# Row gathers of a graph stage: five in flight in place of four

## The chip, the cores and the metric

One core of a Trainium2 chip runs the whole kernel in one launch. The time is device microseconds of one execution; three runs of the kernel before took 5215.01 to 5220.03 us, with a median of 5218.09.

## The reference

The input is 32 images of 64 channels and 48 x 48 pixels. Two layers follow one another, and each adds its result to its input.

```python
x = x + conv(ln_c(x), Wc, bc)             # per image: s = relu(xn^T xn)^2 over all pixel pairs; out = s applied to Wc x + bc
t = to_tokens(x)                           # 73728 tokens of 64 numbers
h = (ln_t(t) @ W_gat).reshape(M, HEADS, NUM_EXPERTS)
e = leaky_relu(a_src[src] + a_dst[dst])    # 262144 drawn edges and a loop at each node
alpha = exp(e - segment_max(e, dst)) / segment_sum(...)
agg = segment_sum(h[src] * alpha, dst) + b_gat
scores = layernorm(agg).mean over heads    # 4 experts, the best 2 taken, softmax weights
out = t + sum over experts of g * (gelu(x @ W1 + b1) @ W2 + b2)
```

The edges are sorted by destination on the chip, so that each maximum and each sum over a destination is a scan along a sorted row. For each edge the row of its source node (24 numbers: 16 of h, 4 of a_src, 4 of a_dst) has to be fetched by an index.

## The kernel before, in words

The program is written out by engine: each of PE, DVE, ACT, POOL and SP has its own list of instructions, and they meet on semaphores. Three parts follow one another.

- `weave` does the first 8 images and sorts the edges between their steps; `merge_nodes` merges the loops into the sorted edges. Drawn edges only name nodes of the first 8 images.
- `flow` does the other 24 images. Meanwhile POOL fetches the source rows of all edges. This is `gather_rows`: 2048 gathers (line 984), each of which takes 128 rows of 96 bytes from the table `htab_d` in HBM by 128 indices and puts them into the tile `rows`. 64 gathers make a chunk; 32 chunks alternate between two halves of `rows`. After the tenth gather of a chunk (`EARLY`) `store_rows` (line 963) writes the chunk before it to `raw_d` in HBM.
- At most `IN_FLIGHT` gathers may be on their way: gather t waits until gather t - IN_FLIGHT has landed (line 983). Gather t counts on semaphore `landed[t % IN_FLIGHT]`, so each place has its own. A store waits on all of them.

When 28 chunks are fetched, POOL waits for the end of the images (`img_done`, line 1730), which SP announces at line 1642, and then works through 32 segments. For each, `segment_rows` issues two large gathers: `got` (line 1724), the segment's edges from `raw_d`, and its neighbour `nb` (line 1726), rows of its nodes from `htab_d`. After each pair it does up to 13 (`PIECE`) of the 256 row gathers that are left; they last for 20 segments. `got` of segment k also waits until ACT has laid out the segment before the last (`a_got`).

For each segment ACT lays out `nb` and `got` (lines 2117 and 2118), and DVE runs the segment's scans, which end with the scan `S` (line 2519). Behind the last segment come a small correction (PE's transposes at lines 1924 and 1929, on semaphore `pe_tails`) and the last stage: for each image POOL fetches 18 times 128 rows (`R`, line 1769), DVE and ACT make gates of them, and PE runs the experts. The expert biases are transposed on PE at line 1919 as soon as the images are done, and DVE copies them at line 2453; they had a semaphore of their own, `pe_b`.

Of the kernel before, what the change touches and what calls it, by code (L numbers as in the profile page):

```python
# [25 lines left out]
FAR = 1.0e6  # L26
FIRST = 8
MIRROR = 40959
IN_FLIGHT = 4
EARLY = 10  # L30
OPENING = 48
KEPT = 49152
# [10 lines left out]
def kernel_program(nc, x, Wc, bc, Wg, att_s, att_d, b_gat, gamma, beta, W1, b1, W2, b2, edges, out):  # L43
# [32 lines left out]
    with ExitStack() as ctx:  # L76
# [7 lines left out]
        def sem(name):  # L84
            return ctx.enter_context(nc.semaphore(name))
# [32 lines left out]
        n.j_in = [sem("j_in0"), sem("j_in1")]  # L118
        n.landed = [sem(f"landed{f}") for f in range(IN_FLIGHT)]
        n.raw_out = [sem("raw_out0"), sem("raw_out1")]  # L120
# [25 lines left out]
        with ExitStack() as sorting:  # L146
            n.big = [sorting.enter_context(nc.sbuf_tensor(f"edges{i}", [P, 2, n.EC], F32)) for i in range(3)]
            weave(nc, n, Wc, bc, Wg, att_s, att_d, edges)
            with ExitStack() as merging:
# [9 lines left out]
                n.slots = mb("slots", [P, n.G * n.W], I32)  # L159
                merge_nodes(nc, n)  # L160
        flow(nc, n, Wc, bc, Wg, att_s, att_d, b_gat, gamma, beta, W1, b1, W2, b2)


# [794 lines left out]
def store_rows(pool, n, k):  # L958
    chunk = n.raw[n.CW:n.E + n.CW, :].rearrange("(k p j) c -> k p (j c)", p=P, j=n.GC)
    end = (k + 1) * n.GC  # L960
    for f in range(IN_FLIGHT):
        pool.wait_ge(n.landed[f], 16 * ((end - f + IN_FLIGHT - 1) // IN_FLIGHT))
    pool.dma_start(chunk[4 * n.G - 1 - k], n.rows[:, k % 2, :, :].rearrange("p j c -> p (j c)")).then_inc(n.raw_out[k % 2], 16)  # L963


def gather_rows(pool, n, t0, t1):
    GC, G, NK = n.GC, n.G, 4 * n.G
    for t in range(t0, t1):
# [11 lines left out]
        if j == 0 and k >= 2:  # L980
            pool.wait_ge(n.raw_out[k % 2], 16 * (k // 2))
        if t >= IN_FLIGHT:
            pool.wait_ge(n.landed[t % IN_FLIGHT], 16 * (t // IN_FLIGHT))
        pool.indirect_dma_start(out=n.rows[:, k % 2, j, :], out_offset=None, in_=n.htabx,  # L984
                                in_offset=bass.IndirectOffsetOnAxis(ap=n.idx[:, g % 2, 3 - c, j:j + 1], axis=0)).then_inc(n.landed[t % IN_FLIGHT], 16)
        if j == EARLY - 1 and k:
# [255 lines left out]
def flow(nc, n, Wc, bc, Wg, att_s, att_d, b_gat, gamma, beta, W1, b1, W2, b2):  # L1242
    B, C, NP, HE, NH, NX = n.B, n.C, n.NP, n.HE, n.NH, n.NX
# [33 lines left out]
    E, M, NT, HID = n.E, n.M, n.NT, n.HID  # L1277
# [19 lines left out]
    with ExitStack() as ctx, ExitStack() as early, ExitStack() as late:  # L1297
# [3 lines left out]
        def sem(name):  # L1301
            return ctx.enter_context(nc.semaphore(name))
# [7 lines left out]
        def ph(name, shape, dt=F32):  # L1310
            return late.enter_context(nc.sbuf_tensor(name, shape, dt))
# [69 lines left out]
        b1r = ph("b1r", [NX, HID])  # L1381
# [44 lines left out]
        up = [late.enter_context(nc.psum_tensor(f"up{i}", [P, 2, 512], F32)) for i in range(GROUP)]  # L1426
# [43 lines left out]
        pe_tails = sem("pe_tails")  # L1470
# [8 lines left out]
        r_free = sem("r_free")  # L1479
        r_in = [sem("r_in0"), sem("r_in1")]  # L1480
        v_set = sem("v_set")
        pe_b = sem("pe_b")
        v_gx = sem("v_gx")
        a_gx = sem("a_gx")
        v_gt = sem("v_gt")
# [287 lines left out]
        def _(pe):  # L1773
# [142 lines left out]
                tokens(B - 1, i)  # L1916
            pe.wait_ge(img_done, 1)
            pe.wait_ge(ew_in, 96)
            pe.transpose(up[0][0:HID, 0, 0:NX], b1r[:, :], n.ident[0:NX, 0:NX]).then_inc(pe_b, 1)
            pe.wait_ge(v_set, 1)  # L1920
            pe.wait_ge(v_tails, 1)
            for k in range(3):
# [41 lines left out]
        def _(act):  # L1964
# [165 lines left out]
                act.activation(state[:, k % 2, :, 0:NC5], S[:, :, :, :].rearrange("p h e j -> p j (h e)"), ACT.Copy)  # L2130
                act.activation(state[:, k % 2, :, NC5:RW], MF[:, :, :].rearrange("p h j -> p j h"), ACT.Copy).then_inc(a_rows, 1)
            for k in range(3):
                act.wait_ge(pe_tails, k + 1)
                act.activation(rt[:, k, :], turn_ps[:, k, :], ACT.Copy).then_inc(a_tails, 1)
            act.wait_ge(v_exp, NK + 1)
            act.activation(ea[:, :, :].rearrange("c a p -> c (a p)"), ex[:, :, :].rearrange("c a p -> c (a p)"), ACT.Exp).then_inc(a_exp, 1)
# [49 lines left out]
        def _(dve):  # L2186
# [262 lines left out]
            norm2(B - 1)  # L2449
            dve.wait_ge(img_done, 1)  # L2450
            dve.wait_ge(ew_in, 96)
            dve.wait_ge(pe_b, 1)
            dve.tensor_copy(b1t[:, :], up[0][0:HID, 0, 0:NX]).then_inc(v_set, 1)
            done = [1]

# [23 lines left out]
            for q in range(G):  # L2479
                par = q % 2  # L2480
                dve.wait_ge(g_in[par], 48 * (q // 2 + 1))
                for c in range(KCH):
                    k = q * KCH + c
# [52 lines left out]
            dve.wait_ge(a_exp, NK + 1)  # L2536
            step(dve.tensor_tensor(ea[:, 1, :], ea[:, 1, :], rt[:, 0, :], ALU.mult))
            dve.tensor_tensor_scan(So[:, 1:G * P + 1], ea[:, 0, :], ea[:, 1, :], 0.0, ALU.mult, ALU.add).then_inc(v_car, 1)
            dve.wait_ge(pe_tails, 4)
            step(dve.tensor_copy(carry[:, :, :, :], back_ps[:, :, :, :]))  # L2540
            dve.sem_inc(v_carry, 1)
            dve.wait_ge(fix_in, 16 * G)
# [154 lines left out]
```

## Time and profile before

| | |
|---|---|
| profiled execution | 5217.17 us |
| its span, first to last instruction | 5214.9 us |
| busy: PE, DVE, ACT, POOL | 67%, 76%, 65%, 56% |
| chain that ended last, by engine | POOL 39%, issue 14%, DMA 13%, DVE 10% |
| row gathers, line 984 | 2048, 2093.9 us busy, 1022 ns each |
| idle time of POOL before them | 663.8 us |

The span is what the profile sees; the 2.3 us around it belong to the launch. In the chain "issue" is time in which an engine waited for nothing that the profile shows, such as the fixed time between two of POOL's gathers, and a DMA's share is its time from issue to landing. The busy time of a gather on POOL ends when the gather is issued, not when its rows have landed. The idle time before an instruction is told with what ended it.

### The profile page before, as it was taken

The numbers are of one execution on the slowest core, as the hardware profiler recorded it, in microseconds if no ns is written. First come the engines' busy times: TensorE is split into PE (matmuls) and PEld (weight loads), VectorE is DVE, ScalarE is ACT, GpSimd is POOL, SyncE is SP. The second block draws the span as 40 slices with busy tenths as digits, with TensorE's granted clock in tenths as the row PEclk, the third lists the DMA queues.
The fourth block names the chain that finished last, engine by engine and source line by source line (L and its number), as shares of the span: only waits on it lengthen the run. The fifth ranks groups of instructions, "written<-read, shape, count | busy, mean of one in ns | idle before, by whom it ended". The sixth has DMA issues, their size and how long they took to land.

```text
span 5214.9 us, 70585 instructions
## 1 busy us (share of the span) xinstructions
PE 3470.7 (67%) x22687; PEld 1460.3 (28%) x22687; DVE 3969.3 (76%) x5512; ACT 3405.7 (65%) x4010; POOL 2917.5 (56%) x2937
## 2 busy tenths in 40 slices
PE   4888988600399999999999999940000017777777
PEld 1223333200144444444444444420000002222222
DVE  8998988997767767777767665635888948778777
ACT  4787978500587877787778777733555527666666
POOL 6000000048777777777777777777774147666661
PEclk9898999855699999999999999975555558899999
DMA  6100110002122222222222222233545526999997
GB/s 256 42 20 21 25 29 16 13 18 83 21 44 56 53 52 55 56 54 52 60 51 53 60 51 51 53 59 116 177 166 195 171 73 144 150 156 165 160 156 153
DMA packets 322231, 441.88 MB, mean 85 GB/s; under 512 B 185241, under 2 KB 251676, under 8 KB 321260
## 3 DMA queue, kind: packets, MB, share of 16 engines
q1 hardware_dynamic: 199504, 288.13, 21.1%
q0 software_dynamic: 105536, 148.61, 16.8%
q10 hardware_dynamic: 16896, 1.18, 0.2%
q8 instruction: 187, 3.06, 0.2%
q14 instruction: 108, 0.88, 0.1%
HBM read 252.35 MB, written 166.47 MB: 80 GB/s over the span
## 4 chain that ended last, share of the span: by engine, by line
POOL 39%; issue 14%; DMA 13%; DVE 10%; SPq 1%; PE 1%; ACT 0%; DVEq 0%; POOLq 0%; ACTq 0%
POOL rows L984 35%; DMA rows<-htab_d,idx 6%; DMA gs<-gates_d 5%; POOL R L1769 2%; DVE ms L2641 1%; DVE pairs L2648 1%; DVE S L2519 1%; SPq L1680 1%; DVE AD L2504 1%; DVE AE L2498 1%; POOL nb L1726 1%; DVE total L2650 0%; POOL got L1724 0%; PE ye L1941 0%; POOL raw_d L963 0%
## 5 line engine op out<-in xcount | busy, mean ns | idle before, releaser
L984 POOL DMA_INDIRECT rows<-htab_d,idx x2048 | 2093.9, 1022 | 663.8 <-issue 606.5
L2073 ACT ACTIVATE rel<-gram 128x1024 f32<-128x1024 f32 (+1 forms) x1080 | 1003.1, 933 | 350.5 <-PE gram L1885 344.1
L2418 DVE SCALAR_TENSOR_TENSOR s<-gram,rel 128x1024 f32<-128x1024 f32 (+1 forms) x720 | 793.3, 1117 | 559.9 <-ACT rel L2073 543.3
L1839 PE MATMUL acc<-s,gT 128*64 128x512 f32 (+1 forms) x4320 | 1031.4, 554 | 0.4 <-issue 0.4
L1885 PE MATMUL gram<-hl 128*64 128x512 f16 (+1 forms) x4320 | 798.2, 366 | 108.9 <-DVE s L2418 65.4
L1885 PE MATMUL gram<-hl,lh 128*64 128x512 f16 (+1 forms) x4320 | 788.1, 362 | 0.0
L1769 POOL DMA_INDIRECT R<-seg_d,nidx x576 | 591.0, 1026 | 194.2 <-issue 168.8
L1084 POOL IOTA slots<- 64x2048 int32 x1 | 1.8, 1832 | 974.1 <-POOLq L192 974.1
L1941 PE MATMUL ye<-hid,w 128*64 128x384 f32 x1536 | 353.7, 538 | 285.4 <-DVE ms L2641 166.5
L2165 ACT ACTIVATE hid<-up,b1t 128x768 f32<-128x768 f32 x384 | 335.7, 899 | 254.2 <-PE up L1953 226.2
L1924 PE MATMUL tailsT<-ident,tails 128*20 128x128 f32 x24 | 5.2, 412 | 731.2 <-DVE tails L2527 731.2
L910 ACT ACTIVATE w_s2r<-w_gram 128x1024 f32<-128x1024 f32 (+1 forms) x360 | 348.1, 967 | 93.9 <-PE w_gram L779 93.4
L316 DVE TENSOR_TENSOR edges<-edges 128x2048 f32<-128x2048 f32 (+1 forms) x186 | 370.7, 1993 | 46.6 <-ACT edges L939 40.9
L1885 PEld LDWEIGHTS gram<-hl 128*64 128x64 f16 x4320 | 251.5, 110 | 515.0 <-DVE s L2418 219.0
L1953 PE MATMUL up<-tne,w 64*128 64x384 f32 x1536 | 373.2, 565 | 7.8 <-DMA x2e<-x_d 7.1
L317 DVE TENSOR_TENSOR edges<-edges 128x2048 f32<-128x2048 f32 (+1 forms) x186 | 369.8, 1988 | 0.0
L753 PE MATMUL w_acc<-w_s2r,w_gT 128*64 128x512 f32 (+1 forms) x1440 | 364.3, 585 | 0.6 <-ACT w_s2r L892 0.6
L892 ACT ACTIVATE w_s2r<-w_s2r 128x1024 f32<-128x1024 f32 (+1 forms) x360 | 360.8, 1003 | 0.0
L2077 ACT ACTIVATE s<-rel 128x1024 f32<-128x1024 f32 (+1 forms) x360 | 349.7, 971 | 11.5
L1839 PEld LDWEIGHTS acc<-s,gT 128*64 128x64 f32 x4320 | 304.2, 139 | 156.7 <-issue 5.9
L2641 DVE SCALAR_TENSOR_TENSOR ms<-ye,b2c,gs 128x384 f32<-128x384 f32 x384 | 233.4, 614 | 135.8 <-DMA gs<-gates_d 97.5
L1885 PEld LDWEIGHTS gram<-hl,lh 128*64 128x64 f16 x4320 | 252.4, 111 | 271.8 <-issue 171.6
(372 smaller groups left out, 5404.8 us busy)
## 6 DMA issues: line engine op xcount, KB each, us to landing
gs<-gates_d SPq DMA_DIRECT2D x64, 1152.0 KB
rows<-htab_d,idx POOLq DMA_INDIRECT x2048
seg_d<-state SPq DMA_DIRECT2D x32, 996.0 KB, 4.2
raw_d<-w_zeros POOLq DMA_DIRECT2D x48, 512.0 KB, 23.2
raw_d<-rows POOLq DMA_DIRECT2D x32, 768.0 KB
tne<-tn_d SPq DMA_DIRECT2D x64, 288.0 KB
x2e<-x_d SPq DMA_DIRECT2D x64, 288.0 KB
out<-res SPq DMA_DIRECT2D x64, 288.0 KB, 8.4
```

The lines of the kernel that those rows point to most:

```text
L316: dve.tensor_tensor(lo, a, b, ALU.min)
L317: step(dve.tensor_tensor(hi, a, b, ALU.max))
L753: last = pe.matmul(acc[(b + c) % 2][j * C:(j + 1) * C, 0:w], gT[:, b % 2, 2 * k + j, :], s2(s)[:, j * w:(j + 1) * w], start=k == 0, stop=k ...
L892: act.activation(s2(s)[:, 0:2 * w], rel(s)[:, 0:2 * w], ACT.Square).then_inc(a_s2, 1)
L984: pool.indirect_dma_start(out=n.rows[:, k % 2, j, :], out_offset=None, in_=n.htabx, in_offset=bass.IndirectOffsetOnAxis(ap=n.idx[:, g % 2, ...
L1769: pool.indirect_dma_start(out=R[:, par, j, :], out_offset=None, in_=n.seg, in_offset=bass.IndirectOffsetOnAxis(ap=nidx[:, par, j:j + 1], a ...
L1839: last = pe.matmul(acc[(par + c) % 2][j * C:(j + 1) * C, 0:w], gT[:, par, 2 * k + j, :], s2[:, u % SLOTS, j * w:(j + 1) * w], start=k == 0 ...
L1885: last = pe.matmul(bank[h * C:(h + 1) * C, j, 0:w], word[:, par, first_pixel:first_pixel + C], hl[:, par, o:o + w], start=own_words, stop= ...
L1941: last = pe.matmul(y[i % 2][h * C:(h + 1) * C, 0:EW], w2[:, k, :], hid[:, i % GROUP, h, :], start=True, stop=True)
L1953: last = pe.matmul(up[i % GROUP][:, h, 0:EW], w1[rows_, k, :], tne[rows_, par, cp * EW:(cp + 1) * EW], start=True, stop=True)
L2073: act.activation(rel[:, t % RELS, 0:2 * w].rearrange("p (j x) -> p j x", j=2), gram[(par + t) % 2][:, :, 0:w], ACT.Relu, scale=1.0 / SPLIT ...
L2418: dve.scalar_tensor_tensor(halves(s2[:, t % SLOTS, 0:2 * w]), gram[(par + t) % 2][:, :, 0:w], 1.0 / SPLIT ** 2, halves(rel[:, t % RELS, 0: ...
```

## The change

The number of gathers in flight goes from 4 to 5. Each place keeps its own semaphore, so there is one more `landed`; the semaphore `pe_b` is taken away, and the transposed biases are counted as the first increment of `pe_tails`. Whoever counted on `pe_tails` waits for one more.

```diff
-IN_FLIGHT = 4
+IN_FLIGHT = 5
...
-        pe_b = sem("pe_b")
...
-            pe.transpose(up[0][0:HID, 0, 0:NX], b1r[:, :], n.ident[0:NX, 0:NX]).then_inc(pe_b, 1)
+            pe.transpose(up[0][0:HID, 0, 0:NX], b1r[:, :], n.ident[0:NX, 0:NX]).then_inc(pe_tails, 1)
...
-                act.wait_ge(pe_tails, k + 1)
+                act.wait_ge(pe_tails, k + 2)
...
-            dve.wait_ge(pe_b, 1)
+            dve.wait_ge(pe_tails, 1)
...
-            dve.wait_ge(pe_tails, 4)
+            dve.wait_ge(pe_tails, 5)
```

The instructions keep their order on every engine; only what they wait for differs. Around the first raw store POOL's list before reads as follows (line, operation, out<-in, partitions x elements):

```order
195 L984 DMA rows<-htab_d,idx 128x24 [waits landed0]
196 L984 DMA rows<-htab_d,idx 128x24 [waits landed1]
197 L963 DMA raw_d<-rows 128x1536 [waits landed2,landed3,landed1,landed0]
198 L984 DMA rows<-htab_d,idx 128x24 [waits landed2]
199 L984 DMA rows<-htab_d,idx 128x24 [waits landed3]
```

And in the changed kernel:

```order
195 L984 DMA rows<-htab_d,idx 128x24 [waits landed3]
196 L963 DMA raw_d<-rows 128x1536 [waits landed3,landed2,landed4,landed1,landed0]
197 L984 DMA rows<-htab_d,idx 128x24 [waits landed4]
198 L984 DMA rows<-htab_d,idx 128x24 [waits landed0]
199 L984 DMA rows<-htab_d,idx 128x24 [waits landed1]
```

The places in flight go round by five in place of four, and the store names five semaphores. Nothing stands elsewhere than before (the numbers differ by one because the first gathers, which wait for nothing, are listed in one row).

## Rows read from the trace of the kernel before

**Rows 1.** The chain that ended last, shares of the span by line.

```profile
POOL rows L984 35%; DMA rows<-htab_d,idx 6%; DMA gs<-gates_d 5%; POOL R L1769 2%; DVE ms L2641 1%; DVE pairs L2648 1%; DVE S L2519 1%; SPq L1680 1%; DVE AD L2504 1%; DVE AE L2498 1%; POOL nb L1726 1%; DVE total L2650 0%; POOL got L1724 0%; PE ye L1941 0%; POOL raw_d L963 0%
```

**Rows 2.** Groups of POOL: count | busy us, mean ns | idle before, releasers.

```profile
L984 POOL DMA_INDIRECT rows<-htab_d,idx x2048 | 2093.9, 1022 | 663.8 <-issue 606.5 <-DMA rows<-htab_d,idx 57.3
L1769 POOL DMA_INDIRECT R<-seg_d,nidx x576 | 591.0, 1026 | 194.2 <-issue 168.8 <-POOL nidx L1765 25.5
...
L674 POOL DMA_DIRECT2D raw_d<-w_zeros x48 | 25.5, 540 | 0.3 <-POOL w_zeros L669 0.3
L963 POOL DMA_DIRECT2D raw_d<-rows x32 | 19.8, 618 | 2.0 <-DMA rows<-htab_d,idx 1.9
```

**Rows 3.** Waits of POOL, 1124 to 3553 us: total us, times, longest.

```profile
POOL rows L984 <- issue: 533.7, 1723, 2.8
POOL rows L984 <- DMA rows<-htab_d,idx: 40.2, 69, 3.1
```

**Rows 4.** Waits of POOL in the segment stretch, 3553 to 3972 us.

```profile
POOL rows L984 <- issue: 73.1, 240, 0.3
POOL rows L984 <- DMA rows<-htab_d,idx: 17.1, 17, 2.0
```

**Rows 5.** Groups of POOL in the segment stretch, raw stores.

```profile
L963 POOL DMA_DIRECT2D raw_d<-rows x5 | 2.9, 585 | 1.9 <-DMA rows<-htab_d,idx 1.9
```

**Rows 6.** Timeline of POOL: start us, us, what [idle before <-releaser].

```profile
1846.88 0.94 POOL L984 DMA_INDIRECT rows<-htab_d,idx  x1 [0.30 <-issue]
...
1854.45 0.94 POOL L984 DMA_INDIRECT rows<-htab_d,idx  x1 [2.88 <-DMA rows<-htab_d,idx]
```

**Rows 7.** The chain in order of time: start us, us to the landing.

```profile
1846.88 7.31 DMA rows<-htab_d,idx
```

**Rows 8.** Windows: us, busy by engine, PEclk, DMA share, GB/s.

```profile
1840.00:1856.00 16.00, 15.83 (x126) 7.36 (x122) 6.23 (x7) 13.05 (x16) 10.07 (x12) 1.00 0.71 130
```

**Rows 9.** Timeline of POOL: the first and last of eleven long gaps.

```profile
1295.77 0.94 POOL L984 DMA_INDIRECT rows<-htab_d,idx  x1 [2.50 <-DMA rows<-htab_d,idx]
...
3920.64 0.94 POOL L984 DMA_INDIRECT rows<-htab_d,idx  x1 [2.02 <-DMA rows<-htab_d,idx]
```

**Rows 10.** Timeline of POOL in the segment stretch.

```profile
3553.52 0.94 POOL L1724 DMA_INDIRECT got<-raw_d,edge  x1 [0.30 <-issue]
...
3595.60 0.94 POOL L1724 DMA_INDIRECT got<-raw_d,edge  x1 [0.30 <-issue]
3596.84 2.19 POOL L1726 DMA_INDIRECT nb<-htab_d,node  x1 [0.30 <-issue]
...
3616.20 0.94 POOL L1724 DMA_INDIRECT got<-raw_d,edge  x1 [0.30 <-issue]
...
3825.20 1.11 POOL L1724 DMA_INDIRECT got<-raw_d,edge  x1 [0.30 <-issue]
...
3835.11 0.94 POOL L984 DMA_INDIRECT rows<-htab_d,idx  x1 [1.90 <-DMA rows<-htab_d,idx]
...
3846.78 1.11 POOL L1724 DMA_INDIRECT got<-raw_d,edge  x1 [0.30 <-issue]
...
3971.49 1.29 POOL L1724 DMA_INDIRECT got<-raw_d,edge  x1 [0.30 <-issue]
```

**Rows 11.** Timeline of DVE: the copy of the transposed biases.

```profile
3474.86 0.16 DVE L2453 COPY b1t<-up 128x4 f32<-128x4 f32 x1 [15.87 <-PE up L1919]
```

**Rows 12.** Waits of ACT and DVE, 3481 to 4210 us: total us, times, longest.

```profile
ACT AE L2117 <- DMA nb<-htab_d,node: 176.3, 21, 80.3
...
DVE AE L2498 <- ACT AE L2117: 131.4, 21, 82.0
```

**Rows 13.** Timeline of SP: its first DMA behind the end of the images.

```profile
3466.72 0.37 SPq L1643 DMA_DIRECT2D pos<-xpos_d  x1
```

**Rows 14.** Timeline of DVE: the last scan of two segments in a row.

```profile
4016.92 3.62 DVE L2519 TENSOR_TENSOR_SCAN S<-G 128x1660 f32<-128x1660 f32 x1
...
4035.32 3.62 DVE L2519 TENSOR_TENSOR_SCAN S<-G 128x1660 f32<-128x1660 f32 x1
```

## The prediction

> **What bounds the kernel now.** I read the views in this order: chain, groups of POOL, waits by stretch, timeline.
>
> The chain that ended last goes through the row gathers of POOL [rows 1]: 35% of the span is their own time and 6% their landings. The groups of POOL [rows 2] say how that looks: 2048 gathers, 2093.9 us busy and 663.8 us idle before them, together 2757.7 us, one every 1.25 us where nothing disturbs (0.94 busy, 0.30 until the next one starts, as in [rows 6]). In the waits of both stretches [rows 3, 4] POOL's gathers wait for no image and not for DVE: they follow one another at POOL's own pace, or wait for a landing. So for more than half of the span POOL is the bound, and PE is beside the path.
>
> How much idle time is more than the fixed gap? In the segment stretch 240 gaps that no landing ended take 73.1 us [rows 4], 0.3046 us each; that is the price of an issue. Up to 3553 us there are 1792 gathers with 533.7 + 40.2 = 573.9 us of idle time [rows 3]; 1792 x 0.3046 is 545.8, and the first gather of all waits 2.5 us more for something else (the longest of the first row, 2.8). That leaves **25.6 us**. In the segment stretch 257 gathers have 90.2 us [rows 4], and 257 x 0.3046 is 78.3: **11.9 us**. Together 37.5 us are waits for the gather four places back, and no depth can win more there.
>
> How such a wait looks: the gather that starts at 1846.88 lands 7.31 us later [rows 7], in a stretch in which the 16 DMA engines are busy 0.71 of the time [rows 8]. The gather four places on could have started at 1851.87 and starts at 1854.45, 2.88 us after the one before it ended [rows 6].
>
> A page of the Trainium skill has another price: DMA: Bandwidth & Descriptors, section Anatomy of one DMA — SWDGE (gpsimd) path, gives a fixed 2.0 us and the bytes over 436e3 per us, an estimate of 2.03 us for the 128 rows of 96 bytes of one gather. By it none would wait for one that started 5 us earlier, and the change would win 0; the trace disagrees with it here, with 7.31 us.
>
> **The change part by part.**
>
> *Five in flight.* No instruction is moved or added on any engine; each gather waits for the one five places back. A late landing therefore holds POOL up one gather later, and each wait shrinks by one spacing, 1.25 us. A gap up to 0.30 + 1.25 = 1.55 us becomes a plain one; a longer one keeps what is above that. Eleven gaps are longer, 1.77 to 3.08 us (the first and the last of them in time: [rows 9]), 25.8 us in sum. Seven lie before 3553 us (18.3 us, of which 7.4 are left) and four behind it (7.5 us, 1.3 left). Gain up to 3553 us: 25.6 - 7.4 = **18.2 us**. The ends of this term: all 25.6, if the long gaps turn out to have had more slack around them, and half, 9.1, if several gathers in a row land late, so that the next one waits in place of the first. I take 18.2, as it comes from the gaps one by one.
>
> *The segment stretch* pays differently. Waits alone would give 11.9 - 1.3 = 10.6. But its intervals have two shapes [rows 10]. From 3595.60 to 3616.20 a segment takes 20.60 us without any wait, because its neighbour gather takes 2.19 us and so gives the large load before it time to drain. From 3825.20 to 3846.78 it takes 21.58, with a gap of 1.90. If every interval takes the first shape, the 20 of them from 3553.52 to 3971.49 (418.0 us) become 20 x 20.60, less the 4 gathers that the last one lacks (5.0), plus 5 raw stores of 0.89 each (0.59 and a gap) and the 1.9 that the last store waits [rows 5]: 413.3, a gain of 4.7. Both shapes are in the rows, so I take the middle of 4.7 and 10.6, **7.6 us**.
>
> *The raw stores* wait on five semaphores in place of four. When a store comes, ten gathers of the next chunk have been issued, and the last of them has waited for the fifth, so all that the store asks for has landed. It takes 618 ns on the mean, a DMA issue of POOL without waits 540 [rows 2]: four waits cost at most 0.08 us, one 0.02, and 32 stores **0.6 us**; the ends are 0 and 32 x 0.08 = 2.5 us. The last store still waits for the last landing.
>
> *The biases* are counted on another semaphore: nothing. The copy that waits for them ran at 3474.86 [rows 11], and nothing on its engine matters until the first segment's rows land: ACT waits up to 80.3 us for those and DVE up to 82.0 [rows 12]. The later users wait for a count that is higher by one, by an increment long past.
>
> **Does the gain reach the end?** Three covers. First, POOL may not take segment rows before the images are done; SP passes that point before 3466.72 [rows 13], 87 us before POOL comes at 3553.52, and 18 of those are used up. Second, DVE needs 18.40 us per segment where it alone sets the pace [rows 14]; the new pace of POOL, 20 to 20.6, stays above, so a saving on POOL shifts DVE. Third, the twelve segments behind the last gather and the gating behind them start that much earlier and last as long as before.
>
> Sum: 18.2 + 7.6 - 0.6 = 25.2 us. The profiled execution took 5217.17 us, 0.9 below the median of the runs shown: 5217.2 - 25.2 = **5192 us**.
>
> **The rivals.**
>
> *Segments give it back.* As POOL's phase against DVE moves, more gathers in the segment stretch are long ones, and that stretch wins nothing: 5217.2 - 18.2 + 0.6 = 5199.6. For: a wait and a neighbour gather of 2.19 us replace one another in [rows 10]. Against: the first shape is still 1 us shorter than the second. Chance 0.13.
>
> *No gain.* The fifth gather finds the queue as late as the fourth did: in a busy stretch the transfers and not the depth set when POOL goes on, and the wait only changes its place. 5217 us. For: a late gather lands 7.31 us after its start, nearly six spacings. Against: only 69 of 1792 gaps were ended by a landing [rows 3], so the queue catches up soon after each. Chance 0.07. The page's price above ends at 5217 too, by its own reason (there would be no landing to wait for); the trace's landings leave that 0.02.
>
> *Slower.* Gathers that wait less meet more of DVE's instructions and are longer themselves. An undisturbed one takes 0.94 us, these 1022 ns on the mean; the gathers of the last stage, 18 in a row that wait for no landing, take 1026 [rows 2]. If the mean rose by 12 ns, over 2048 gathers 25 us, all would be given back; 25 ns more, a third of today's excess of 78, would give 5217.2 - 25.2 + 51.2 = 5243. Against: the gathers that wait for nothing show only 4 ns more. Chance 0.04. The Trainium skill (SBUF — State Buffer, section SBUF: two separate sides) states that some DVE instructions lock POOL out of writing a DMA's descriptors; no row here shows that depth makes that worse.
>
> **How the numbers follow.** Forecast 0.74, at 5192. Segments give it back 0.13, no gain 0.09 with the page's reason, slower 0.04. About 0.2% (10.4 us) is what a measurement here tells from no change; the forecast and the first rival are faster by more than that: faster 0.87, same 0.09, slower 0.04. Low end: all 37.5 us go, 5179.7, and a little of the runs' spread, 5179. High end: 9.1 of the first term, 4.7 of the second, less 2.5, gives 11.3 us and 5206; I stop at 5204, since all three ends at once are unlikely.
>
> **What would show it.** In the new profile the gathers' idle time should fall from 663.8 to some 635 us with their mean near 1022 ns; fewer gaps should be ended by a landing, the longest near 1.8 us; the first segment gather should stand near 3535 and the last near 3946, in place of 3553.52 and 3971.49, with DVE's segments behind it still 18.4 us apart. A mean above 1034 ns, or as much idle time as now, would prove me wrong.

## The result, and the profile after

The changed kernel takes **5173.16 us** (median of 6 runs, 5164.83 to 5182.84) where the kernel before takes 5215.44 (5208.35 to 5220.03): ratio 0.992, with a 95% interval of 0.9904 to 0.9936. That is 42.3 us less. The forecast was 5192.0 with a range from 5179: the sign was right, and the mechanism as far as waits go, but the gain came out larger than anything the range allowed for. Two later series of the same kernel gave 0.9939 and 0.9923; the mean of the three ratios is 0.9927, some 38 us. One execution of e2 (8633.6 us) and one of e5 (5348.5 us) came at a granted clock of 0.44 and 0.77 where the others of their kernels had some 0.85, and are left out of the medians below.

The profiled execution of after took 5168.96 us with a span of 5166.7, before 5214.9: 48.2 us less. The groups of POOL of the changed kernel, over the whole span (columns as in [rows 2]; R is line 1768 here, as the lines behind `pe_b` moved up by one):

```profile
L984 POOL DMA_INDIRECT rows<-htab_d,idx x2048 | 2091.6, 1021 | 637.8 <-issue 610.8 <-DMA rows<-htab_d,idx 27.0
L1768 POOL DMA_INDIRECT R<-seg_d,nidx x576 | 591.5, 1027 | 196.1 <-issue 170.3 <-POOL nidx L1764 25.5 <-DVEq L2592 0.3
...
L674 POOL DMA_DIRECT2D raw_d<-w_zeros x48 | 25.5, 540 | 0.3 <-POOL w_zeros L669 0.3
L963 POOL DMA_DIRECT2D raw_d<-rows x32 | 19.8, 618 | 2.0 <-issue 1.9
```

Against [rows 2], the idle time before the 2048 gathers fell from 663.8 to 637.8 us (forecast: some 635), their mean from 1022 to 1021 ns (forecast: near 1022), and the raw stores kept their 618 ns to the digit. By these rows alone the forecast looks complete. The whole-span mean hides two opposite movements, which show when the same view is cut in two. Kernel before, groups of POOL from the first gather up to the segments, then in the segment stretch:

```profile
L984 POOL DMA_INDIRECT rows<-htab_d,idx x1792 | 1835.6, 1024 | 573.9 <-issue 533.7 <-DMA rows<-htab_d,idx 40.2
...
L984 POOL DMA_INDIRECT rows<-htab_d,idx x256 | 258.3, 1009 | 90.0 <-issue 72.8 <-DMA rows<-htab_d,idx 17.1
L1726 POOL DMA_INDIRECT nb<-htab_d,node x20 | 32.5, 1626 | 6.1 <-issue 6.1
L1724 POOL DMA_INDIRECT got<-raw_d,edge x21 | 21.5, 1023 | 6.4 <-issue 6.4
```

The same view of the changed kernel:

```profile
L984 POOL DMA_INDIRECT rows<-htab_d,idx x1792 | 1822.4, 1017 | 556.8 <-issue 537.4 <-DMA rows<-htab_d,idx 19.4
...
L984 POOL DMA_INDIRECT rows<-htab_d,idx x256 | 269.2, 1052 | 81.0 <-issue 73.4 <-DMA rows<-htab_d,idx 7.6
L1723 POOL DMA_INDIRECT got<-raw_d,edge x21 | 23.0, 1097 | 6.4 <-issue 6.4
L1725 POOL DMA_INDIRECT nb<-htab_d,node x20 | 20.0, 1002 | 6.1 <-issue 6.1
```

In front of the segments the idle time fell by 17.1 us, and the gathers themselves by 13.2, from 1024 to 1017 ns: nothing in the forecast stood for those 13.2. In the segment stretch the idle time fell by 9.0, the neighbour gathers by 12.5, and the row gathers grew by 10.9. Waits of POOL in the changed kernel, first gather to first segment (total us, times, longest), to be held against [rows 3]:

```profile
POOL rows L984 <- issue: 537.4, 1747, 2.8
...
POOL rows L984 <- DMA rows<-htab_d,idx: 19.4, 45, 1.8
```

45 gaps are ended by a landing where there were 69. By the working of the prediction (1792 gaps of 0.3046 us and 2.5 for the first are 548.3) the waits were 25.6 us and are 8.5. Single waits did not all shrink as the forecast said. The timeline of POOL in the changed kernel, at the place of [rows 6]:

```profile
1853.99 0.94 POOL L984 DMA_INDIRECT rows<-htab_d,idx  x1 [0.30 <-DMA rows<-htab_d,idx]
1857.53 0.94 POOL L984 DMA_INDIRECT rows<-htab_d,idx  x1 [2.59 <-issue]
```

A long gap stands there again, but it is 2.59 us and not 2.88 - 1.25 = 1.63. Over all of them the shrinking still sums up nearly as forecast.

The segment stretch, on POOL's timeline of the changed kernel:

```profile
3524.80 0.94 POOL L1723 DMA_INDIRECT got<-raw_d,edge  x1 [0.30 <-issue]
...
3689.07 1.16 POOL L1723 DMA_INDIRECT got<-raw_d,edge  x1 [0.30 <-issue]
3690.53 1.12 POOL L1725 DMA_INDIRECT nb<-htab_d,node  x1 [0.31 <-issue]
3691.95 0.94 POOL L984 DMA_INDIRECT rows<-htab_d,idx  x1 [0.30 <-issue]
3693.20 1.59 POOL L984 DMA_INDIRECT rows<-htab_d,idx  x1 [0.30 <-issue]
...
3709.58 1.04 POOL L1723 DMA_INDIRECT got<-raw_d,edge  x1 [0.31 <-issue]
...
3933.86 1.25 POOL L1723 DMA_INDIRECT got<-raw_d,edge  x1 [0.30 <-issue]
```

The first segment gather stands at 3524.80 (forecast near 3535) and the twenty-first, the last of [rows 10], at 3933.86 (forecast near 3946). The 20 intervals take 409.1 us in place of 418.0 [rows 10]. The one from 3689.07 to 3709.58 is neither of the two shapes of [rows 10]: 20.51 us, a short neighbour gather (1.12) and a long row gather behind it.

Behind POOL, the last scans of two segments in a row on DVE's timeline of the changed kernel, which answer to [rows 14]:

```profile
3979.28 3.62 DVE L2518 TENSOR_TENSOR_SCAN S<-G 128x1660 f32<-128x1660 f32 x1
...
3997.69 3.62 DVE L2518 TENSOR_TENSOR_SCAN S<-G 128x1660 f32<-128x1660 f32 x1
```

They are 18.41 us apart, as before (18.40), so the cover of DVE held.

Of the 48.2 us of this pair of executions, then: 30.2 are won up to the first segment gather (17.1 of waits, 13.2 of gathers), 8.9 in the segments, and 10.7 in the last stage, from its first gather to the end (971.1 before, 960.4 after); 1.6 are lost ahead of the gathers, which start at 1126.44 and not at 1124.89. Two of these terms were not in the forecast, the shorter gathers and the last stage. The experiments ask which of them the change brings.

### The profile page after: what moved, and what is told of

Read it like the earlier page. It is cut to its first block and busy times, and to the rows that moved or that the text cites. A ratio compares the mean times of both kernels' runs of the same rounds, so it can differ in the third digit from the quotient of the medians.

```text
span 5166.7 us, 70585 instructions
## 1 busy us (share of the span) xinstructions
PE 3463.7 (67%) x22687; PEld 1457.9 (28%) x22687; DVE 3968.2 (77%) x5512; ACT 3404.9 (66%) x4010; POOL 2904.6 (56%) x2937
## 5 line engine op out<-in xcount | busy, mean ns | idle before, releaser
L984 POOL DMA_INDIRECT rows<-htab_d,idx x2048 | 2091.6, 1021 | 637.8 <-issue 610.8
L316 DVE TENSOR_TENSOR edges<-edges 128x2048 f32<-128x2048 f32 (+1 forms) x186 | 370.7, 1993 | 48.0 <-ACT edges L939 42.3
```

The source lines that it names most:

```text
L316: dve.tensor_tensor(lo, a, b, ALU.min)
```

## The experiments

Three readings stood against each other: the waits and the segments carry the gain and the rest is scatter; waiting itself makes gathers long, so that fewer waits make them shorter; the gathers are short or long by where POOL's rhythm of 1.25 us falls among DVE's instructions, and another number in flight only moves it.

In each trace three stretches were measured: the first 1792 gathers, the 20 segment intervals, and the last stage. The kernel before ran again on each of the chips used; each ratio is against its executions there.

**The changed kernel again**, for a second trace.

> The changed kernel once more, for a second trace. Theory A (the waits went as forecast, and what was won beyond that are gathers that are no longer lengthened by DVE): the stretch from the first row gather to the first segment gather takes 2398 us again, within 6, and the gathers' busy time 2092, within 6; the stretch of the last stage, from its first gather to the end, comes out anywhere from 958 to 975, since it has nothing to do with the change. Theory B (the last stage too is shorter by the change): 960 us there again, within 2, against 971 in the kernel before.

5180.97 us, ratio 0.9939 (0.9922 to 0.9956). The first 1792 gathers are busy 1821.3 us, as short as in the first profile, and the segments take 409.0; but the last stage takes 975.5 us, longer than in the kernel before. So the shorter gathers come back and the 10.7 us of the last stage do not:

```profile
L984 POOL DMA_INDIRECT rows<-htab_d,idx x1792 | 1821.3, 1016 | 559.9 <-issue 540.1 <-DMA rows<-htab_d,idx 19.8
```

**The biases alone**: all of the change but the number in flight.

```diff
-IN_FLIGHT = 5
+IN_FLIGHT = 4
```

> Four in flight as before, only the biases counted on the semaphore of the tails. Theory A: no change, 5215 us within 0.15%, the first segment gather near 3553. The rival that the bias count is a part of the gain: under 5205.

5209.28 us, 0.9999 (0.9987 to 1.001). The count of the biases does nothing.

**Five in flight in one stretch only**, in front of the segments (e3), or in the segments only (e4, with the 4 and the 5 exchanged). `AHEAD_ROWS` is 1792.

```diff
-        if t >= IN_FLIGHT:
-            pool.wait_ge(n.landed[t % IN_FLIGHT], 16 * (t // IN_FLIGHT))
+        back = t - (5 if t < AHEAD_ROWS else 4)
+        if back >= 0:
+            pool.wait_ge(n.landed[back % IN_FLIGHT], 16 * (back // IN_FLIGHT + 1))
```

> Five semaphores, but a gather waits for the one five places back only in the first 1792, for the one four places back in the segment stretch. Theory A: the first segment gather near 3525 as with five everywhere, the segment stretch from first to twenty-first segment gather 418 us as before, in all 5215 - 30 = 5185. Rival (five win only in the segment stretch, the rest is scatter between runs): 5205 or more.

> The other half: four places back in the first 1792 gathers, five in the segment stretch. Theory A: first segment gather near 3553, segment stretch 409 us in place of 418, in all 5206. Rival (segments alone bring more than a third of the 42 us): under 5200.

e3: 5191.88 us, 0.9958 (0.9945 to 0.9972), 7 us above what was expected. e4: 5207.02 us, 0.9984 (0.9972 to 0.9996). 22.2 and 7.1 us below the 5214.07 of the kernel before on that chip; the two together, 29.2, come near the 33.1 of the whole change there. In e3 the segments, with four again, take 420.4 us; in e4, with five, 407.6. The first 1792 gathers are busy 1826.7 us in e3 and 1830.8 in e4. So both stretches win on their own, and the front wins three quarters. The row gathers and the neighbour gathers of the segment stretch, in e3 and then in e4 (whose view holds one neighbour gather more):

```profile
L986 POOL DMA_INDIRECT rows<-htab_d,idx x256 | 258.6, 1010 | 90.8 <-issue 72.8 <-DMA rows<-htab_d,idx 18.0
L1727 POOL DMA_INDIRECT nb<-htab_d,node x20 | 33.7, 1687 | 6.1 <-issue 6.1
```

```profile
L986 POOL DMA_INDIRECT rows<-htab_d,idx x256 | 269.6, 1053 | 79.3 <-issue 74.7 <-DMA rows<-htab_d,idx 4.7
L1727 POOL DMA_INDIRECT nb<-htab_d,node x21 | 20.8, 991 | 6.4 <-issue 6.4
```

The longer row gathers, the shorter neighbour gathers and the shorter waits come with five in the segments, and go with four.

**Eight in flight.** Three semaphores were made free by counting their events on others, as the change does with the biases; two of the places stand here.

```diff
-IN_FLIGHT = 5
+IN_FLIGHT = 8
...
-            pe.wait_ge(v_car, 1)
+            pe.wait_ge(v_tails, 2)
...
-            dve.wait_ge(gc_in, 48)
+            dve.wait_ge(ew_in, 144)
```

> Eight in flight, each on its own semaphore (three more increments are counted on semaphores that are there already). Theory A (a wait for a landing costs its own time and, through the place in the image at which it lets POOL go on, lengthens gathers that then meet DVE's instructions of each second image): no waits over 0.33 us are left, the first 1792 gathers are busy for 1815 to 1824 us as with five, not 1832 as with four, the first segment gather comes 2388 us after the first row gather, the segment stretch takes 405 to 410 us, in all 10 us under the kernel with five. Rival (the shorter gathers with five are chance, the sign is open): busy time back at 1828 or more, no gain over five.

5176.46 us, 0.9925 (0.9908 to 0.9942). Groups of POOL of this kernel, gathers up to the segments:

```profile
L984 POOL DMA_INDIRECT rows<-htab_d,idx x1792 | 1826.9, 1019 | 548.6 <-issue 538.5 <-DMA rows<-htab_d,idx 10.1
```

Idle 548.6 against 548.3 of plain gaps: no wait is left. Yet its time is that of five, and not the 10 us less that was expected. A second series gave 5175.8 us (0.9902 to 0.9932 as a ratio of 0.9917), with 548.5 us idle and 1827.9 busy.

> Eight in flight once more, beside five on the same chip. No waits for landings in both traces of it; theory C: gathers up to the segments 1822 to 1830 us, the segment stretch 411 as before, in all within 6 us of five, since what the last waits cost is met again as longer gathers. Rival (the first look at eight was unlucky): 8 us or more under five.

Some 10 us fewer waits in front of the segments than with five (558.4 on the mean of five traces, below) are partly paid back by gathers that are 3 us longer than the mean with five; the rest is too small to tell. Three series of the changed kernel gave 5173.16, 5180.97 and 5177.82 us: no version tried here clearly beats it.

**Three in flight**, still on five semaphores.

```diff
-        if t >= IN_FLIGHT:
-            pool.wait_ge(n.landed[t % IN_FLIGHT], 16 * (t // IN_FLIGHT))
+        back = t - (3)
+        if back >= 0:
+            pool.wait_ge(n.landed[back % IN_FLIGHT], 16 * (back // IN_FLIGHT + 1))
```

> Five semaphores, each gather waits for the one three places back. Theory A: waits as the landings of the kernel before give them for three places, about 120 us in the whole, so some 85 us more than with four: 5300 us. The rival that waits themselves lengthen gathers: the first 1792 are busy for over 1845 us too.

5327.49 us, 1.0219 (1.0198 to 1.024), 27 us above what was expected. Groups of POOL, the same stretch:

```profile
L985 POOL DMA_INDIRECT rows<-htab_d,idx x1792 | 1824.9, 1018 | 644.1 <-issue 489.9 <-DMA rows<-htab_d,idx 154.1
```

95.8 us of waits (644.1 - 548.3), nearly four times those of four in flight, and the gathers are as short as with five or eight. That speaks against waiting itself as what makes gathers long. Three is 114.6 us slower than the 5212.85 of the kernel before on that chip. Against the trace of before, 70.2 us of it are more waits in front, 10.7 of which the shorter gathers give back, and 52.9 lie in the segments (470.9 us).

**The start moved**: four (e7) and five (e8) in flight, and a memset that stood earlier put ahead of the first gather, twice.

```diff
-            pool.memset(n.fix[:, :, :], 0.0).then_inc(n.f_rdy, 1)
...
+            step(pool.memset(n.fix[:, :, :], 0.0))
+            pool.memset(n.fix[:, :, :], 0.0).then_inc(n.f_rdy, 1)
             gather_rows(pool, n, 0, OPENING)
```

> Four in flight, and two short memsets of POOL (0.27 us each) ahead of the first gather, so that its grid of 1.25 us stands half a step elsewhere against DVE. Theory A (where gathers meet DVE is set again by each wait and each collision): the shift is forgotten, 1832 us within 4 for the first 1792 gathers, in all as before. Rival (chance of the start): the busy time moves by 8 us or more.

> The same two memsets with five in flight. Theory A: 1823 us within 4 for the first 1792 gathers, in all as with five. Rival (chance of the start): back at 1828 to 1836, and half of what five bring in gathers is gone.

e7: 5215.78 us, 1.0003 (0.9991 to 1.0016), gathers busy 1839.6 us, outside what was expected. e8: 5182.9 us, 0.9942 (0.9921 to 0.9962), 1821.1 us busy. But the shift was lost at once. The instruction of DVE that the first gather waits for, and POOL's first two gathers, in the kernel before and then in e7:

```profile
1122.79 0.17 DVE L1208 TENSOR_SCALAR need<-needf 1x32 int32<-1x32 f32 x1
1124.89 1.75 POOL L984 DMA_INDIRECT rows<-htab_d,idx  x1 [2.77 <-issue]
1126.94 1.84 POOL L984 DMA_INDIRECT rows<-htab_d,idx  x1 [0.30 <-issue]
```

```profile
1122.68 0.17 DVE L1209 TENSOR_SCALAR need<-needf 1x32 int32<-1x32 f32 x1
1125.10 1.43 POOL L984 DMA_INDIRECT rows<-htab_d,idx  x1 [1.49 <-issue]
1126.84 1.84 POOL L984 DMA_INDIRECT rows<-htab_d,idx  x1 [0.30 <-issue]
```

Against DVE the first gather begins 2.42 us later in place of 2.10, but it is 0.32 us shorter, and the second begins 4.16 us later where it was 4.15. The same holds of e8 (4.15) and the changed kernel (4.15). So e7 and e8 did not test the start; they are further executions of four and of five, and the difference between four and five stays.

**The rhythm disturbed all along**: four (e9) and five (e10) in flight, with two small memsets that wait for one another ahead of every sixteenth gather (their semaphore is made free as in e5).

```diff
+        if t < 1792 and t % 16 == 15:
+            for _ in range(2):
+                pool.memset(n.nudge[:, :], 0.0).then_inc(n.nudged, 1)
+                n.nudges += 1
+                pool.wait_ge(n.nudged, n.nudges)
```

> Four in flight, with two very short memsets of POOL ahead of each sixteenth of the first 1792 gathers, which move its grid against DVE by some 0.3 us every 20 us and cost some 35 us. Theory C (four is dear because its waits put the grid at a bad place against DVE in image after image; no depth is dear by itself): the gathers' busy time up to the segments falls from 1834 (mean of four traces) to 1822 to 1830. Rival (a wait by itself lengthens the gathers that follow): 1832 or more.

> The same memsets with five in flight. Theory C: 1822 to 1830, within 5 us of the one with four. Rival: 1823 or less, 9 us or more under the one with four.

e9: 5240.11 us, 1.0043 (1.0029 to 1.0057). e10: 5221.04 us, 1.0013 (1.0001 to 1.0026). Groups of POOL of e9, with the memsets:

```profile
L991 POOL DMA_INDIRECT rows<-htab_d,idx x1792 | 1830.6, 1022 | 567.1 <-issue 499.7 <-DMA rows<-htab_d,idx 37.0 <-POOL nudge L988 30.3
L988 POOL MEMSET nudge<- 128x8 f32 x224 | 25.9, 116 | 6.5
```

The same of e10:

```profile
L991 POOL DMA_INDIRECT rows<-htab_d,idx x1792 | 1836.7, 1025 | 554.9 <-issue 509.5 <-POOL nudge L988 30.3 <-DMA rows<-htab_d,idx 15.0
L988 POOL MEMSET nudge<- 128x8 f32 x224 | 26.1, 116 | 7.7 <-DMA rows<-htab_d,idx 1.2
```

The gathers of both were expected at 1822 to 1830 us; neither came there, and the order turned round: now those with five are the longer ones, by 6.1 us. The waits kept their order (567.1 against 554.9 idle, with the same 30.3 of memsets in both). So, as far as one execution of each can tell, shorter gathers are not a property of five in flight; their length moves by some 10 us with whatever places them. The lower waits of five stay with five. The medians are 19.1 us apart (the profiled spans 10.6), where four and five without memsets are some 38 apart.

**The changed kernel a third time**, beside the last three.

> The changed kernel, beside eight on the same chip: 5175 to 5183 us; gathers up to the segments 1823 within 4, segment stretch 409.

5177.82 us, 0.9923 (0.9906 to 0.994); idle 557.4 us, gathers 1828.4 (1 us above what was expected), last stage 975.1.

The traces together, in us (each number the mean of one execution of each kernel named):

| | four in flight | five in flight |
|---|---|---|
| first 1792 gathers, idle (before, e2, e4, e7; after, e1, e3, e8, e12) | 575.7 | 558.4 |
| the same, busy | 1833.8 (1829.1 to 1839.6) | 1824.0 (1821.1 to 1828.4) |
| first gather to first segment gather (the same) | 2429.0 | 2401.9 |
| 20 segment intervals (before, e2, e3, e7, e9; after, e1, e4, e8, e10, e12) | 418.9 | 409.0 |
| last stage (before, e2, e7, e9; after, e1, e8, e10, e12) | 968.8 (964.7 to 973.4) | 968.5 (960.4 to 975.5) |

So the change is worth 17.3 us of waits, 9.8 of shorter gathers and 9.9 in the segments: 37.0 us, which meets the 38 us of the three ratios. The 9.8 us are the least sure of these: the ranges of four and five lie close, and three executions of the changed kernel alone gave 1821.3 to 1828.4. The last stage scatters by 15 us whatever the number is; that the first pair of profiles differed by 10.7 there was scatter. It goes along with the granted clock of TensorE in that stage, here (columns as in [rows 8]) in the first profile of the changed kernel and in the third:

```profile
4206.30:5166.70 960.40, 683.08 (x3060) 204.34 (x3060) 736.08 (x1822) 623.34 (x682) 598.02 (x607) 0.92 0.88 151
```

```profile
4214.00:5189.10 975.10, 690.84 (x3060) 205.85 (x3060) 735.93 (x1822) 624.20 (x682) 601.28 (x607) 0.89 0.88 149
```

The mean granted clock was 0.92 in 960.4 us, 0.91 in the 963.2 of e8, 0.90 in the 971.1 of the kernel before and the 975.5 of e1, and 0.89 in 975.1. What makes it differ is not shown.

Of the three readings, the first holds for the waits and the segments, but the gathers are more than scatter of one pair: they came out shorter in each of the five traces with five in flight and no memsets than in any of the four with four. The second does not fit e6, which has the most waits and gathers as short as five's. The third fits e9 and e10 and what the traces show of single gathers (last section).

## Why the prediction was right and wrong

**The waits in front of the segments** were right: forecast 18.2 us, 17.1 in the first pair and 17.3 on the mean. That the long ones would keep 7.4 us came near (8.5; 10.1 on the mean), though they did not each shrink by 1.25 us: the sum was right, the single gaps were not.

**The step that failed** is one that the sum does not have: the length of the gathers themselves. The prediction took the 0.30 us gap apart to four digits and held the 1022 ns for fixed ("with their mean near 1022 ns"), because the whole-span group has one mean. That mean is 78 ns above an undisturbed gather, 160 us in all over 2048 gathers, over four times the 37.5 us of waits. It was weighed once, in the rival "slower", and only upwards. It went the other way: 9.8 us on the mean of the traces, 13.2 in the first pair. By the traces 8.3 of the 9.8 us lie in gathers that begin while one of three instructions of DVE runs (last section); why they begin at better places with five in flight stays open.

**The low end** failed with it. "All 37.5 us go" bounds the waits and not the change, and "a little of the runs' spread" was 0.7 us where the last stage alone scatters by 15 between executions. With a term of 10 us for the gathers either way the sum would have kept its middle, and the range would have held the 5173.16. What that low end called the most, 37.5 us, is what the three series give on the mean, 38. Between 5192.0 and 5173.16 lie 18.8 us. The means of the table place 11.8 of them: 9.8 of gathers, 2.3 more in the segments and 0.6 of stores, less 0.9 of waits. Another 1.7 are the base, as the profiled execution of the kernel before (5217.17 us) lay that much above the median of its six. The other 5.3 are not placed: this series was the fastest of three, and e1's 5180.97 us lies inside the range.

**The segments** were right in size: 7.6 us forecast between 4.7 and 10.6, 8.9 in the first pair and 9.9 on the mean. They got there another way, so the sum was met in part by luck. "Every interval takes the first shape" did not happen, nor did the waits go alone: the neighbour gathers became short, the row gathers long, and most gaps plain. The working counts 257 gathers in this stretch where there are 256, which moves its 11.9 us by 0.1.

**The raw stores** cost 0 and not 0.6 (618 ns both times). **The biases** cost nothing, as forecast; e2 shows it alone. **The covers** held: the gain reached the end, with 18.41 us from segment to segment on DVE, and SP, whose first DMA behind the images stands here:

```profile
3465.44 0.37 SPq L1642 DMA_DIRECT2D pos<-xpos_d  x1
```

That is still 59 us ahead of POOL's 3524.80 in the changed kernel.

**The rivals.** "No gain" is refuted by every series of five against four, e10 against e9 among them. "Segments give it back" is refuted by e4: five there alone win 7.1 us. "Slower" had a real mechanism, as [rows 2] suggested, with the wrong sign for this placing; with eight, where no gather in front of the segments is held up by a landing, they are at 1019 to 1020 ns there, and over all 2048 at 1026 and 1024, not at the 1034 from which that rival would have decided. Its mechanism does act between e9 and e10, where five's gathers are the longer ones, and takes 6 us of five's gain there. The 2.03 us for a landing, an estimate from the Trainium skill's page DMA: Bandwidth & Descriptors (section Anatomy of one DMA — SWDGE (gpsimd) path), disagrees with these runs too: with three in flight a gather asks for one that began 3.75 us before it, so by that estimate three would have cost nothing, and they cost 114.6 us.

## What to carry to other kernels

Waits that a deeper queue can remove are well counted gap by gap, against the plain gap of the same trace. But when an engine's pace is the bound, a mean duration that stands above the undisturbed one is a term of the sum as well, with both signs, and it has to be read stretch by stretch, since one group over the whole span can hide a fall and a rise that cancel. A low end must bound the time and not one mechanism's waits, and two traces of one pair cannot tell a stage's gain from that stage's scatter: a second execution of the same kernel did. And a disturbance has to be looked for in the trace before its result is read: that of e7 and e8 was gone at the second gather.

## What the hardware showed

How a gather becomes long can be followed at one place. POOL's timeline of the kernel before:

```profile
2092.73 0.94 POOL L984 DMA_INDIRECT rows<-htab_d,idx  x1 [0.30 <-issue]
2093.98 2.06 POOL L984 DMA_INDIRECT rows<-htab_d,idx  x1 [0.30 <-issue]
```

DVE's timeline of the kernel before, at that moment:

```profile
2093.86 1.36 DVE L2371 TENSOR_TENSOR vr<-cv,rstd 128x1152 f32<-128x1152 f32 x1
```

The gather begins 0.12 us behind an instruction of DVE with two inputs in SBUF, which ends at 2095.22; the gather ends at 2096.04, after 2.06 us, 0.82 us behind DVE's end. The same place in the changed kernel, POOL and then DVE:

```profile
2092.13 1.10 POOL L984 DMA_INDIRECT rows<-htab_d,idx  x1 [0.30 <-issue]
2093.53 1.09 POOL L984 DMA_INDIRECT rows<-htab_d,idx  x1 [0.30 <-issue]
```

```profile
2092.09 0.32 DVE L2366 TENSOR_SCALAR step_s<-step_d 128x328 f32<-128x328 uint8 x1
2092.45 1.36 DVE L2370 TENSOR_TENSOR vr<-cv,rstd 128x1152 f32<-128x1152 f32 x1
```

Here the gather begins 1.08 us behind the start of the same instruction. It ends at 2094.62, again 0.81 us behind DVE's end at 2093.81, and takes only 1.09 us. The gather ahead of it begins 0.04 us behind another instruction of DVE, which ends at 2092.41, and ends 0.82 us behind that. The Trainium skill (SBUF — State Buffer, section SBUF: two separate sides) describes an exclusive lock: the one that starts first, of a DVE instruction with two SBUF inputs and a GpSimd instruction that reads SBUF, has the port pair until it ends. This place agrees for a gather that begins behind such an instruction of DVE. It does not for one that begins ahead: the instruction at 2092.45 begins while the gather of 2092.13 runs, and takes the same 1.36 us as in the kernel before.

It is not the only place. In the trace of the kernel before, 75 of the first 1792 gathers begin while one of three such instructions runs, each of which comes once an image (`vr`, `t` and `tk`, lines 2371, 2404 and 2288). Of these 72 end 0.81 to 0.85 us behind it, wherever in it they began; the other three begin within 0.03 us of its start and take 0.94 us. What the 75 take above 0.94 us is 48.9 us. Over the traces it is 47.8 us on the mean with four in flight (44.3 to 52.7) and 39.5 with five (37.4 to 42.0), in the same executions as in the first row of the table: 8.3 of the 9.8 us by which five's gathers are shorter. With the memsets it is 46.3 us in e9 and 49.1 in e10, 2.8 of 6.1. So collisions of this kind make up most of the 10 us between the kernels; why four's places are the dearer ones without the memsets, and the cheaper ones with them, stays open.

Two numbers more were not expected. From three to eight in flight the time goes 5327, 5215, some 5178 and some 5176 us: the step from three to four is three times that from four to five, and behind five there is nothing left that these runs can tell. And the last stage, which the change does not touch, differed by up to 15 us between executions with the same code in it, 0.3% of the kernel; the longer it took, the lower as a rule was the clock granted in it (0.92 to 0.89).
